# Attention: denominators of unmasked key tiles from sums made in pairs on GpSimd

## The chip, the cores and the metric

The kernel runs on one core of a Trainium2 chip. The metric is the device time of one launch in microseconds. Engines are TensorE (PE; PEld is its weight load), VectorE (DVE), ScalarE (ACT), GpSimd (POOL) and SyncE (SP), whose queue issues nearly all transfers.

## What is computed

Two blocks of a sequence model over 2 x 1024 tokens of 512 channels: a time mix, a feed-forward layer, then causal attention with 16 heads of 32 channels, then a mixture of eight experts, each followed by a layer norm. The change is in attention:

```python
scores = jnp.einsum('bhqd,bhkd->bhqk', q, k) / np.sqrt(D)
scores = jnp.where(causal, scores, -jnp.inf)
attn = jax.nn.softmax(scores, axis=-1)
out = jnp.einsum('bhqk,bhkd->bqhd', attn, v).reshape(b, t, c)
```

and, beside it, in the preparation of the experts' weights, which the reference takes as `w_gate.astype(jnp.bfloat16)` and so on.

## The kernel before

Every stage is written out by hand, one function per engine; an engine's instructions run in the order of the text, and semaphores order the engines among each other. Attention is `attend` (line 1718). It works on 8 **units**: 2 batches x 4 groups of 4 heads. The scores stand transposed: keys on partitions, queries on columns. A unit has 12 **steps** (`STEPS`, line 1725): for the first 512 queries key tiles 0 to 3 (steps 0 to 3), for the second 512 key tiles 0 to 7 (steps 4 to 11). Steps 0 to 3 and 8 to 11 meet the diagonal: they are cut to 512, 384, 256 and 128 columns and need a mask. Steps 4 to 7 are whole and unmasked.

For every step and head (`h`, four of them):

- TensorE makes scores (`scores`, line 1886, matmul L1893) into one of three banks `st`, and between them the pieces of `mx.piece` (L1286), scores of the next units whose row maxima VectorE takes (L1298, L1301).
- ScalarE takes the exponential into `pt` (`exps`, L1861), a ring of `PT` = 3 buffers of 128 x 4 x 512 floats.
- GpSimd masks the diagonal block of steps that need it (`affine_select`, L1843).
- Two steps later (`LAG` = 2) TensorE multiplies `pt` by the values into `num` and by a block of ones into `den` (`pv`, L1911); the second product sums the exponentials over the keys. A product is four matmuls of 32 rows, one per head.

At steps 3 and 11 ends a half; ScalarE copies `den` and `num` out (L1852, L1853), VectorE divides (L1937, L1940), SP stores.

Beside this the stage prepares the experts' weights for the next one (`NarrowWeights`, line 1998): 24 pieces, three per unit, each loaded as 32-bit floats (`load`, L2023), cast to bf16 by GpSimd (`narrow`, L2029) and stored (`store`, L2035). Three buffers `raw` and three `cast` go round, piece n uses buffer n % 3. SP's order in unit u (lines 1795 to 1815): the seven loads of the keys, queries and values of unit u + 2 (`mx.load`, L1256, none from unit 6 on) once the products of the unit before are done; then for each of three pieces the store of the piece of unit u - 1 and the load of that of unit u; the store of results, the rows of negated maxima for unit u + 1 (L1266), a store of results. A load waits for the cast that frees `raw`, which is one unit old; a cast waits for the load and for the store that frees `cast`. On GpSimd the three casts of a unit stand at step 4, ahead of the masks of steps 8 to 11:

```python
for s in range(NS):
    if s == TT:
        for n in range(PER_UNIT):
            narrow.narrow(pool, u * PER_UNIT + n)
    if diag(s) is None:
        continue
    pool.wait_ge(exp_done, (u * NS + s + 1) * HG)
```

Of the kernel before, what the change touches and what calls it, by code (L numbers as in the profile page):

```python
# [9 lines left out]
ALU = mybir.AluOpType  # L10
# [4 lines left out]
BF16 = mybir.dt.bfloat16  # L15
U32 = mybir.dt.uint32

P = 128
# [1699 lines left out]
def attend(nc, a, src, dst, o_out, mx, ow, result):  # L1718
# [8 lines left out]
    DIAGS = sum(j >= qc * TT for qc, j in STEPS)  # L1727
    LAST_PIECES, TURN_STEP, FRONT = 8, 9, 12
    LAG = 2
    PT = LAG + 1  # L1730
    ST = 3
    DIVIDE_CHUNKS = 4
    CHUNK = TB // DIVIDE_CHUNKS
# [3 lines left out]
    with Bench(nc, "at_") as b:  # L1737
# [13 lines left out]
        o_stored = [b.sem(f"o_stored{s}") for s in range(QC)]  # L1751
        narrow = NarrowWeights(nc, b, a)
        PER_UNIT = len(narrow.pieces) // UNITS
        out = Outcome(b, src, dst, o_out, o_stored, ow, mx, st[0], ((UNITS - 2) * NS, (UNITS - 1) * NS))
        banks = [num, mx.bank[0]], [den, mx.bank[1]], [mx.bank[2], st[0]], [st[1], st[2]]
        expert_sync, expert_gpsimd, expert_scalar, expert_tensor, expert_vector = experts(
# [68 lines left out]
        @block.gpsimd  # L1825
        def _(pool):
            pool.memset(ones[:, :], 1.0).then_inc(ones_small_set, 1)
            pool.wait_ge(ones_small_set, 1)
            mx.set_ones(pool, SLOTS - 1)
            pool.wait_ge(mx.ones_set, SLOTS)  # L1830

            for u in range(UNITS):
                for s in range(NS):
                    if s == TT:
                        for n in range(PER_UNIT):
                            narrow.narrow(pool, u * PER_UNIT + n)
                    if diag(s) is None:
                        continue
                    pool.wait_ge(exp_done, (u * NS + s + 1) * HG)
                    part = pt[:, s % PT, :, diag(s):diag(s) + P]  # L1840
                    alone(pool)

                    pool.affine_select(out=part, in_=part, compare_op=ALU.is_ge, fill=0.0, base=0,  # L1843
                                       pattern=[[0, HG], [1, P]], channel_multiplier=-1).then_inc(masked, 1)
            expert_gpsimd(pool)

        @block.scalar
        def _(act):
# [6 lines left out]
            def exps(u, s):  # L1855
                off = diag(s) or 0

                at_least(act, pv_done, u * NS + s - LAG)
                for h in range(HG):
                    act.wait_ge(scores_done, (u * NS + s) * HG + h + 1)  # L1860
                    act.activation(pt[:, s % PT, h, off:TB], st[(s * HG + h) % ST][:, off:TB], ACT.Exp,  # L1861
                                   scale=SCALE).then_inc(exp_done, 1)
# [22 lines left out]
        def _(pe):  # L1885
# [13 lines left out]
            def pv(u, s):  # L1899
                qc, kt = STEPS[s]  # L1900
                off = diag(s) or 0
                pe.wait_ge(exp_done, (u * NS + s + 1) * HG)
                if diag(s) is not None:
                    pe.wait_ge(masked, u * DIAGS + diags(s) + 1)
                if kt == 0:
                    at_least(pe, copied, (u * QC + qc) * 2)
                first, last = kt == 0, s in ENDS
                for total, lhs in ((num, None), (den, ones)):
                    for h in range(HG):
                        rows = slice(h * HD, (h + 1) * HD)  # L1910
                        mm = pe.matmul(total[rows, off:TB], vv[u % SLOTS][:, kt, rows] if lhs is None else lhs[:, :],  # L1911
                                       pt[:, s % PT, h, off:TB], start=first, stop=last, skip_group_check=True)
                mm.then_inc(pv_done, 1)

            pe.wait_ge(ones_small_set, 1)
            for g in range(UNITS * NS):
                u, s = place(g)
                if s == 0:
                    pe.wait_ge(mx.ones_set, min(u + 1, SLOTS))
                    pe.wait_ge(mx.rows_loaded, (u + 1) * 2 * DMA)  # L1920
                scores(u, s)
                if g >= LAG:
                    pv(*place(g - LAG))
                if s == TURN_STEP and u + 1 < UNITS:
                    mx.turn(pe, u + 1)
            for g in range(UNITS * NS - LAG, UNITS * NS):
# [71 lines left out]
class NarrowWeights:  # L1998
# [5 lines left out]
    def __init__(self, nc, b, a):  # L2004
# [1 line left out]
        self.gu = nc.dram_tensor("expert_gu_bf", [EXPERTS, P, 2, KT * INNER], BF16, kind="Internal").ap()  # L2006
        self.d = nc.dram_tensor("expert_d_bf", [EXPERTS, P, NM * C], BF16, kind="Internal").ap()
        self.a = a
        self.raw = [b.sb(f"raw{s}", [P, NM * C]) for s in range(self.BUFFERS)]
        self.cast = [b.sb(f"cast{s}", [P, NM * C], BF16) for s in range(self.BUFFERS)]  # L2010
        self.loaded = [b.sem(f"loaded{s}") for s in range(self.BUFFERS)]
        self.stored = [b.sem(f"stored{s}") for s in range(self.BUFFERS)]
        self.narrowed = b.sem("narrowed")
# [3 lines left out]

    def load(self, sp, n):
        e, g = self.pieces[n]
        sp.wait_ge(self.narrowed, n - self.BUFFERS + 1) if n >= self.BUFFERS else None  # L2020
        source = self.a["expert_gu"][e][:, g].rearrange("p k n -> p (k n)") if g < 2 \
            else self.a["expert_d"][e].rearrange("p m n -> p (m n)")
        sp.dma_start(self.raw[n % self.BUFFERS][:, 0:self.cols(n)], source).then_inc(self.loaded[n % self.BUFFERS], DMA)  # L2023

    def narrow(self, pool, n):
        s = n % self.BUFFERS
        pool.wait_ge(self.loaded[s], (n // self.BUFFERS + 1) * DMA)
        at_least(pool, self.stored[s], (n // self.BUFFERS) * DMA)
        pool.tensor_copy(self.cast[s][:, 0:self.cols(n)], self.raw[s][:, 0:self.cols(n)]).then_inc(self.narrowed, 1)  # L2029

    def store(self, sp, n):
# [961 lines left out]
```

## Time and profile before

| | us |
|---|---|
| median of 3 runs | 1600.88 (1598.05 to 1601.29) |
| the profiled execution | 1599.74 |
| its span, first to last instruction | 1598.0 |
| PE busy | 1489.6 (93%) |
| DVE busy | 990.5 (62%) |
| ACT busy | 613.4 (38%) |
| POOL busy | 459.8 (29%) |
| mean granted TensorE clock | 0.975 of full speed |

Attention takes the time from 939 to 1281 us of the span. All rows below are from the one profiled execution. A busy time is the union of a group's instructions. A wait in brackets is the idle time of the engine ahead of an instruction and what ended it; the share of busy time says little about who waits for whom.

### The profile page before, as it was taken

The numbers are of one execution on the slowest core, as the hardware profiler recorded it, in microseconds if no ns is written. First come the engines' busy times: TensorE is split into PE (matmuls) and PEld (weight loads), VectorE is DVE, ScalarE is ACT, GpSimd is POOL, SyncE is SP. The second block draws the span as 40 slices with busy tenths as digits, with TensorE's granted clock in tenths as the row PEclk, the third lists the DMA queues.
The fourth block names the chain that finished last, engine by engine and source line by source line (L and its number), as shares of the span: only waits on it lengthen the run. The fifth ranks groups of instructions, "written<-read, shape, count | busy, mean of one in ns | idle before, by whom it ended". The sixth has DMA issues, their size and how long they took to land. (4 is left out here: it accounts for less than half of the span.)

```text
span 1598.0 us, 22563 instructions
## 1 busy us (share of the span) xinstructions
PE 1489.6 (93%) x7696; PEld 1084.6 (68%) x7696; DVE 990.5 (62%) x1916; ACT 613.4 (38%) x1079; POOL 459.8 (29%) x385
## 2 busy tenths in 40 slices
PE   6999889999999999999998989999999898897996
PEld 4787768788888888888876764444444376674554
DVE  4977967854545554552432757777777375466664
ACT  4343444623422431341211025554555634231554
POOL 0433343302421440340432122221222224003760
PEclk9999989999999999999999989999999998998998
DMA  5111536503321430424257573666662566712336
GB/s 184 44 62 53 189 112 226 195 27 130 94 66 40 145 104 0 132 79 160 110 184 232 172 201 106 177 177 190 191 187 100 201 255 226 289 56 70 102 98 224
DMA packets 105182, 223.40 MB, mean 140 GB/s; under 512 B 9281, under 2 KB 35265, under 8 KB 104193
## 3 DMA queue, kind: packets, MB, share of 16 engines
q1 hardware_dynamic: 101344, 211.96, 40.9%
q0 software_dynamic: 3744, 10.23, 2.1%
q8 instruction: 55, 0.90, 0.2%
q14 instruction: 39, 0.31, 0.1%
HBM read 157.54 MB, written 64.36 MB: 139 GB/s over the span
## 5 line engine op out<-in xcount | busy, mean ns | idle before, releaser
L1861 ACT ACTIVATE at_pt<-at_st 128x512 f32<-128x512 f32 (+3 forms) x384 | 164.2, 497 | 140.4 <-PE at_st L1893 139.6
L898 POOL TENSOR_TENSOR ff_w_lo<-ff_raw,ff_w_hi 128x1024 fp32r<-128x1024 f32 x64 | 153.8, 2405 | 210.8 <-ACT ff_w_hi L928 210.8
L115 PE MATMUL op_bank<-ff_x_hi,ff_w_lo 128*128 128x512 f32 x512 | 200.2, 391 | 0.0
L117 PE MATMUL op_bank<-ff_x_hi,ff_w_hi 128*128 128x512 f32 x512 | 200.0, 391 | 0.0
L116 PE MATMUL op_bank<-ff_x_lo,ff_w_hi 128*128 128x512 f32 x512 | 199.9, 391 | 0.0
L1159 DVE TENSOR_TENSOR ff_h_lo<-ff_hf,ff_h_hi 128x512 f32 (+1 forms) x64 | 149.6, 2337 | 53.6 <-ACT ff_h_hi L1047 53.3
L1893 PE MATMUL at_st<-mx_qp,mx_kp 98*128 98x512 f32 (+3 forms) x288 | 104.4, 395 | 15.9 <-ACT at_pt L1861 10.6
L928 ACT ACTIVATE ff_w_hi<-ff_raw 128x1024 fp32r<-128x1024 f32 x64 | 67.8, 1061 | 118.3 <-PE op_bank L117 116.0
L115 PEld LDWEIGHTS op_bank<-ff_x_hi,ff_w_lo 128*128 128x128 f32 x512 | 96.7, 189 | 20.3
L116 PEld LDWEIGHTS op_bank<-ff_x_lo,ff_w_hi 128*128 128x128 f32 x512 | 96.7, 189 | 20.2
L117 PEld LDWEIGHTS op_bank<-ff_x_hi,ff_w_hi 128*128 128x128 f32 x512 | 96.6, 189 | 20.4
L1893 PEld LDWEIGHTS at_st<-mx_qp,mx_kp 98*128 98x128 f32 x288 | 54.8, 198 | 74.5 <-issue 34.8
L1298 DVE CUSTOM_DVE_ANT_0 mx_mx<-mx_mx,mx_mask 128x256 f32<-128x256 f32 (+3 forms) x172 | 83.0, 490 | 29.7 <-PE mx_mx L1286 28.5
L115 PE MATMUL mx_mx<-ff_down_hi,ff_h_lo 128*128 128x512 f32 x256 | 100.3, 392 | 0.0
L117 PE MATMUL mx_mx<-ff_down_hi,ff_h_hi 128*128 128x512 f32 x256 | 99.8, 390 | 0.0
L116 PE MATMUL mx_mx<-ff_down_lo,ff_h_hi 128*128 128x512 f32 x256 | 99.6, 389 | 0.0
L1151 DVE SCALAR_TENSOR_TENSOR ff_hf<-op_bank,ff_sc,ff_hf 128x512 f32<-128x512 f32 x64 | 48.0, 750 | 72.0 <-PE op_bank L117 70.5
L1843 POOL TENSOR_SCALAR_AFFINE_SELECT at_pt<-at_pt 128x512 f32<-128x512 f32 x64 | 41.3, 649 | 156.8 <-ACT at_pt L1861 156.6
L1286 PE MATMUL mx_mx<-mx_kp,mx_qp 96*128 96x512 f32 (+1 forms) x208 | 75.8, 371 | 9.9 <-DMA mx_vv<-v_tokens 4.4
L1301 DVE TENSOR_REDUCE mx_tops<-mx_mx 128x1 f32<-128x512 f32 x100 | 68.7, 687 | 24.9 <-PE mx_mx L1286 24.7
L1911 PE MATMUL at_den<-at_pt,at_ones 128*32 128x512 f32 (+3 forms) x768 | 82.9, 504 | 0.0
L1040 ACT ACTIVATE ff_hf<-op_bank,ff_sc 128x512 f32<-128x512 f32 x64 | 44.0, 688 | 82.6 <-PE op_bank L117 82.6
(450 smaller groups left out, 3352.8 us busy)
## 6 DMA issues: line engine op xcount, KB each, us to landing
ff_raw<-in_Wug SPq DMA_DIRECT2D x64, 512.0 KB, 3.6
at_raw<-in_expert_gu SPq DMA_DIRECT2D x16, 704.0 KB, 12.2
mx_qp<-q_hi SPq DMA_DIRECT2D x12, 512.0 KB, 5.6
mx_kp<-k_hi SPq DMA_DIRECT2D x12, 512.0 KB, 11.3
at_raw<-in_expert_d SPq DMA_DIRECT2D x8, 768.0 KB, 14.2
expert_gu_bf<-at_cast SPq DMA_DIRECT2D x16, 352.0 KB, 10.9
ex_e_gu<-expert_gu_bf SPq DMA_DIRECT2D x8, 704.0 KB, 8.4
tm_raw_x<-in_xT SPq DMA_DIRECT2D x4, 1024.0 KB, 6.4
```

Source lines behind the costliest of these rows:

```text
L115: pe.matmul(out, cut_l(ll), cut_r(rh), start=first, stop=False, **kw)
L116: pe.matmul(out, cut_l(lh), cut_r(rl), start=False, stop=False, **kw)
L117: return pe.matmul(out, cut_l(lh), cut_r(rh), start=False, stop=last, **kw)
L898: pool.tensor_tensor(w[j][1][:, :, :, :], raw[:, j], f32(w[j][0][:, :, :, :]), ALU.subtract)\
L928: act.activation(w[j][0][:, :, :, :], raw[:, j], ACT.Copy).then_inc(w_hi_ready, 1)
L1159: dve.tensor_tensor(h_lo[:, bass.ds(n + j, 1), :], hf[:, j:j + 1, :], f32(h_hi[:, bass.ds(n + j, 1), :]), ALU.subtract).then_inc(h_lo_read ...
L1286: pe.matmul(bank[:, 0:hi - lo], self.qp[j][0:R_MAX, h, qt * P:(qt + 1) * P], self.kp[j][0:R_MAX, h, lo:hi], start=True, stop=True).then_in ...
L1298: dve.tensor_tensor_reduce(piece, piece, self.mask[:, TB - (hi - lo):], 1.0, -3e38, ALU.add, ALU.max, out)\
L1301: dve.reduce_max(out, piece, AX.X).then_inc(self.piece_read, 1)
L1861: act.activation(pt[:, s % PT, h, off:TB], st[(s * HG + h) % ST][:, off:TB], ACT.Exp, scale=SCALE).then_inc(exp_done, 1)
L1893: pe.matmul(st[(s * HG + h) % ST][:, off:TB], kp[j][0:ROWS, h, kt * P:(kt + 1) * P], qp[j][0:ROWS, h, qc * TB + off:(qc + 1) * TB], start= ...
L1911: mm = pe.matmul(total[rows, off:TB], vv[u % SLOTS][:, kt, rows] if lhs is None else lhs[:, :], pt[:, s % PT, h, off:TB], start=first, sto ...
```

## The change

In the four unmasked steps of a unit the exponentials are no longer multiplied by ones step by step. GpSimd adds those of steps 4 and 5, and of steps 6 and 7, into one buffer `pair_sum` (128 x 4 x 512), and TensorE multiplies each sum by ones once (`total_pair`), after the products that go with step 7 and with step 10. The ring `pt` has four buffers. A mask or a new exponential may not take a buffer whose sum is still to be made: `exps` waits for `summed` from step 8 on. The second sum waits for the product of the first (`totalled`), since `pair_sum` is one buffer.

To make room, each `cast` buffer of the weights is laid over its `raw` buffer. So a load may no longer start when the cast before is done, but when the store before has landed.

```diff
--- before.py
+++ after.py
@@ -1727,7 +1727,11 @@
     DIAGS = sum(j >= qc * TT for qc, j in STEPS)
     LAST_PIECES, TURN_STEP, FRONT = 8, 9, 12
     LAG = 2
-    PT = LAG + 1
+    PT = LAG + 2
+    PAIR_STEPS = [(TT, TT + 1), (TT + 2, TT + 3)]
+    SUM_AT = {step: n for n, (_, step) in enumerate(PAIR_STEPS)}
+    TOTAL_AT = {TT + 3: 0, TT + 6: 1}
+    SUMS = len(PAIR_STEPS)
     ST = 3
     DIVIDE_CHUNKS = 4
     CHUNK = TB // DIVIDE_CHUNKS
@@ -1751,6 +1755,8 @@
         o_stored = [b.sem(f"o_stored{s}") for s in range(QC)]
         narrow = NarrowWeights(nc, b, a)
         PER_UNIT = len(narrow.pieces) // UNITS
+        pair_sum = b.sb("pair_sum", [P, HG, TB])
+        summed, totalled = b.sem("summed"), b.sem("totalled")
         out = Outcome(b, src, dst, o_out, o_stored, ow, mx, st[0], ((UNITS - 2) * NS, (UNITS - 1) * NS))
         banks = [num, mx.bank[0]], [den, mx.bank[1]], [mx.bank[2], st[0]], [st[1], st[2]]
         expert_sync, expert_gpsimd, expert_scalar, expert_tensor, expert_vector = experts(
@@ -1834,6 +1840,14 @@
                     if s == TT:
                         for n in range(PER_UNIT):
                             narrow.narrow(pool, u * PER_UNIT + n)
+                    if s in SUM_AT:
+                        n = u * SUMS + SUM_AT[s]
+                        first, second = PAIR_STEPS[SUM_AT[s]]
+                        pool.wait_ge(exp_done, (u * NS + second + 1) * HG)
+                        at_least(pool, totalled, n)
+                        pool.tensor_tensor(pair_sum[:, :, :], pt[:, first % PT, :, :], pt[:, second % PT, :, :], ALU.add)\
+                            .then_inc(summed, 1)
+                        pool.wait_ge(summed, n + 1)
                     if diag(s) is None:
                         continue
                     pool.wait_ge(exp_done, (u * NS + s + 1) * HG)
@@ -1855,7 +1869,9 @@
             def exps(u, s):
                 off = diag(s) or 0
 
-                at_least(act, pv_done, u * NS + s - LAG)
+                at_least(act, pv_done, u * NS + s - PT + 1)
+                if s >= 2 * TT:
+                    act.wait_ge(summed, u * SUMS + (s - 2 * TT) // 2 + 1)
                 for h in range(HG):
                     act.wait_ge(scores_done, (u * NS + s) * HG + h + 1)
                     act.activation(pt[:, s % PT, h, off:TB], st[(s * HG + h) % ST][:, off:TB], ACT.Exp,
@@ -1906,11 +1922,20 @@
                     at_least(pe, copied, (u * QC + qc) * 2)
                 first, last = kt == 0, s in ENDS
                 for total, lhs in ((num, None), (den, ones)):
+                    if lhs is not None and TT <= s < 2 * TT:
+                        continue
                     for h in range(HG):
                         rows = slice(h * HD, (h + 1) * HD)
                         mm = pe.matmul(total[rows, off:TB], vv[u % SLOTS][:, kt, rows] if lhs is None else lhs[:, :],
                                        pt[:, s % PT, h, off:TB], start=first, stop=last, skip_group_check=True)
                 mm.then_inc(pv_done, 1)
+
+            def total_pair(u, n):
+
+                pe.wait_ge(summed, u * SUMS + n + 1)
+                for h in range(HG):
+                    mm = pe.matmul(den[h * HD:(h + 1) * HD, :], ones[:, :], pair_sum[:, h, :], start=n == 0, stop=False, skip_group_check=True)
+                mm.then_inc(totalled, 1)
 
             pe.wait_ge(ones_small_set, 1)
             for g in range(UNITS * NS):
@@ -1921,6 +1946,8 @@
                 scores(u, s)
                 if g >= LAG:
                     pv(*place(g - LAG))
+                if s in TOTAL_AT:
+                    total_pair(u, TOTAL_AT[s])
                 if s == TURN_STEP and u + 1 < UNITS:
                     mx.turn(pe, u + 1)
             for g in range(UNITS * NS - LAG, UNITS * NS):
@@ -2006,8 +2033,12 @@
         self.gu = nc.dram_tensor("expert_gu_bf", [EXPERTS, P, 2, KT * INNER], BF16, kind="Internal").ap()
         self.d = nc.dram_tensor("expert_d_bf", [EXPERTS, P, NM * C], BF16, kind="Internal").ap()
         self.a = a
-        self.raw = [b.sb(f"raw{s}", [P, NM * C]) for s in range(self.BUFFERS)]
-        self.cast = [b.sb(f"cast{s}", [P, NM * C], BF16) for s in range(self.BUFFERS)]
+        homes = []
+        self.raw = []
+        for s in range(self.BUFFERS):
+            homes.append(b.next_at())
+            self.raw.append(b.sb(f"raw{s}", [P, NM * C]))
+        self.cast = [b.overlay(f"cast{s}", [P, NM * C], homes[s], BF16) for s in range(self.BUFFERS)]
         self.loaded = [b.sem(f"loaded{s}") for s in range(self.BUFFERS)]
         self.stored = [b.sem(f"stored{s}") for s in range(self.BUFFERS)]
         self.narrowed = b.sem("narrowed")
@@ -2017,7 +2048,7 @@
 
     def load(self, sp, n):
         e, g = self.pieces[n]
-        sp.wait_ge(self.narrowed, n - self.BUFFERS + 1) if n >= self.BUFFERS else None
+        at_least(sp, self.stored[n % self.BUFFERS], n // self.BUFFERS * DMA)
         source = self.a["expert_gu"][e][:, g].rearrange("p k n -> p (k n)") if g < 2 \
             else self.a["expert_d"][e].rearrange("p m n -> p (m n)")
         sp.dma_start(self.raw[n % self.BUFFERS][:, 0:self.cols(n)], source).then_inc(self.loaded[n % self.BUFFERS], DMA)
@@ -2025,7 +2056,6 @@
     def narrow(self, pool, n):
         s = n % self.BUFFERS
         pool.wait_ge(self.loaded[s], (n // self.BUFFERS + 1) * DMA)
-        at_least(pool, self.stored[s], (n // self.BUFFERS) * DMA)
         pool.tensor_copy(self.cast[s][:, 0:self.cols(n)], self.raw[s][:, 0:self.cols(n)]).then_inc(self.narrowed, 1)
 
     def store(self, sp, n):
```

GpSimd's order in the first unit, from the memset of the constant rows of `kp` to the masks of the second half. The names are the tiles of attention (`at_`); of before:

```order
L1843 AFFINE_SELECT at_pt<-at_pt 128x4x128 x4
L2029 CAST at_cast<-at_raw 128x1408 x2
L2029 CAST at_cast<-at_raw 128x1536
L1843 AFFINE_SELECT at_pt<-at_pt 128x4x128 x8
L2029 CAST at_cast<-at_raw 128x1408 x2
```

and of the change:

```order
L1857 AFFINE_SELECT at_pt<-at_pt 128x4x128 x4
L2059 CAST at_cast_7012<-at_raw 128x1408
L2059 CAST at_cast_7013<-at_raw 128x1408
L2059 CAST at_cast_7014<-at_raw 128x1536
L1848 TENSOR_TENSOR at_pair_sum<-at_pt 128x2048 x2
L1857 AFFINE_SELECT at_pt<-at_pt 128x4x128 x8
```

Both sums stand behind the three casts and ahead of the mask of step 8.

TensorE from the last scores of step 8 to the first piece behind the turned maxima in step 10 (`at_st` are scores, `mx_mx` and `at_mx` pieces); of before:

```order
L1911 MATMUL at_num<-at_pt,mx_vv 32x512 x4
L1911 MATMUL at_den<-at_pt,at_ones 32x512 x4
L1893 MATMUL at_st<-mx_qp,mx_kp 128x384 x4
L1911 MATMUL at_num<-at_pt,mx_vv 32x512 x4
L1911 MATMUL at_den<-at_pt,at_ones 32x512 x4
L1311 MATMUL mx_mx<-mx_ident,mx_tops 32x128
```

and of the change, the end of step 7 and then the same place:

```order
L1929 MATMUL at_num<-at_pt,mx_vv 32x512 x4
L1937 MATMUL at_den<-at_pair_sum,at_ones 32x512 x4
L1909 MATMUL at_st<-mx_qp,mx_kp 128x512
...
L1909 MATMUL at_st<-mx_qp,mx_kp 128x384 x4
L1929 MATMUL at_num<-at_pt,mx_vv 32x512 x4
L1311 MATMUL mx_mx<-mx_ident,mx_tops 32x128
```

The products with ones behind steps 4 to 7 are gone, and the product over the first sum stands between steps 7 and 8.

## Rows read from the trace of the kernel before

**Rows 1.** the page, part 2: busy tenths of TensorE in 40 equal slices.

```profile
PE   6999889999999999999998989999999898897996
```

**Rows 2.** who waited for whom, 939 to 1281 us: us, times, longest us.

```profile
PE at_st L1893 <- ACT at_pt L1861: 12.5, 31, 2.7
PE at_st L1893 <- POOL at_ones L1827: 5.0, 1, 5.0
...
ACT at_pt L1861 <- PE at_st L1893: 139.6, 101, 4.5
```

**Rows 3.** timeline of SP, units 2, 3 and 7: start, us, issue.

```profile
1035.27 0.33 SPq L1256 DMA_DIRECT2D mx_qp<-q_hi  x1
...
1038.98 6.26 SPq L2035 DMA_DIRECT2D expert_gu_bf<-at_cast  x1
...
1047.51 0.43 SPq L2023 DMA_DIRECT2D at_raw<-in_expert_d  x1
...
1077.59 0.32 SPq L1256 DMA_DIRECT2D at_qp<-q_hi  x1
...
1238.65 0.50 SPq L2035 DMA_DIRECT2D expert_gu_bf<-at_cast  x1
```

**Rows 4.** timeline of TensorE, units 0, 2 and 7.

```profile
970.12 0.50 PE L1893 MATMUL at_st<-mx_qp,mx_kp 98*128 98x512 f32 x1
...
1051.02 1.04 PE L1911 MATMUL at_den<-at_pt,at_ones 128*32 128x512 f32 x8
1051.99 0.50 PE L1893 MATMUL at_st<-at_qp,at_kp 98*128 98x512 f32 x1
...
1055.67 0.50 PE L1893 MATMUL at_st<-at_qp,at_kp 98*128 98x512 f32 x1
...
1066.05 1.06 PE L1911 MATMUL at_num<-at_pt,at_vv 128*32 128x512 f32 x8
...
1267.46 0.73 PE L1893 MATMUL at_st<-mx_qp,mx_kp 98*128 98x512 f32 x2
```

**Rows 5.** timeline of GpSimd, units 0, 2 and 6: last column the wait before.

```profile
968.43 1.47 POOL L2029 CAST at_cast<-at_raw 128x1536 bf16<-128x1536 f32 x1 [0.48 <-DMA at_raw<-in_expert_d]
...
1057.61 1.36 POOL L2029 CAST at_cast<-at_raw 128x1408 bf16<-128x1408 f32 x1 [16.36 <-DMA at_raw<-in_expert_gu]
...
1062.97 1.47 POOL L2029 CAST at_cast<-at_raw 128x1536 bf16<-128x1536 f32 x1 [1.39 <-DMA at_raw<-in_expert_d]
1064.39 1.22 POOL L1843 TENSOR_SCALAR_AFFINE_SELECT at_pt<-at_pt 128x512 f32<-128x512 f32 x2
...
1212.14 4.07 POOL L2029 CAST at_cast<-at_raw 128x1408 bf16<-128x1408 f32 x3
```

**Rows 6.** groups by form of GpSimd, whole span: busy us, mean ns.

```profile
L898 POOL TENSOR_TENSOR ff_w_lo<-ff_raw,ff_w_hi 128x1024 fp32r<-128x1024 f32 x64 | 153.8, 2405 | 210.8 <-ACT ff_w_hi L928 210.8
...
L352 POOL TENSOR_TENSOR tm_rw<-tm_num,tm_rec 128x512 f32<-128x512 f32 x16 | 28.7, 1796 | 79.9 <-DVE tm_rec L585 79.9
...
L2297 POOL TENSOR_TENSOR ex_sd_lo<-ex_raw_d,ex_sd_hi 128x1536 fp32r<-128x1536 f32 x1 | 3.5, 3479 | 0.0
```

**Rows 7.** DMA issues of 1038.9 to 1040 us: KB, us to landing.

```profile
expert_gu_bf<-at_cast SPq DMA_DIRECT2D x1, 352.0 KB, 16.9
```

**Rows 8.** DMA issues of unit 6 from 1197.7, then of unit 7 from 1238.6.

```profile
at_raw<-in_expert_gu SPq DMA_DIRECT2D x1, 704.0 KB, 5.1
expert_gu_bf<-at_cast SPq DMA_DIRECT2D x1, 352.0 KB, 2.9
...
expert_gu_bf<-at_cast SPq DMA_DIRECT2D x1, 352.0 KB, 9.4
```

**Rows 9.** the page, part 6: DMA issues.

```profile
ff_raw<-in_Wug SPq DMA_DIRECT2D x64, 512.0 KB, 3.6
```

**Rows 10.** busy time in two stretches: PE, PEld, DVE, ACT, POOL, PEclk, DMA.

```profile
938.00:951.00 13.00, 12.70 (x44) 8.55 (x44) 8.46 (x28) 6.98 (x13) 5.55 (x5) 0.50 0.90 216
1108.00:1113.00 5.00, 4.98 (x24) 1.75 (x23) 3.49 (x10) 0.88 (x3) 0.63 (x1) 0.66 0.15 56
```

## The prediction

> **What bounds the kernel now.** I first read the page's slices [rows 1]: TensorE is busy in eight tenths or more of every slice but the first and two of the last four, also in attention (939 to 1281 us, slices 24 to 33 of 40). TensorE bounds that stage, as far as it has operands. The lists of waits there [rows 2] say that its longest is for the exponentials, 12.5 us in 31 waits; GpSimd is waited for once, 5.0 us at the stage's start. ScalarE waits 139.6 us for scores, in its group of exponentials, and for nothing else of weight. Then I read one unit in time, unit 2 (of 0 to 7), and count from T0, the issue of its first load of keys and queries, 1035.27 [rows 3]; the next unit's is 1077.59, so a unit takes 42.3 us.
>
> In the TensorE timeline [rows 4] a group of products with ones over 512 columns (one matmul per head, four; the row counts eight) starts at 1051.02, and the scores behind it at 1051.99: 0.97 us a group. Scores of step 8 start at 1055.67, T0+20.4. In the GpSimd timeline [rows 5] the three casts of a unit, which stand ahead of all it does from step 4 on, do not follow the mask of step 3. The first starts at 1057.61 after 16.36 us of waiting for its weight piece, and the third ends at 1064.44, T0+29.2. Only then come the masks of steps 8 and 9, which TensorE needs at 1066.05 [rows 4]. So GpSimd is idle a long time and yet **late**, because DMA is late. Nothing waits for it today, by 1.6 us.
>
> **The products.** Per unit four groups with ones go (4 x 0.97 = 3.9 us) and two over the sums come (1.9): 1.9 us saved, 15.5 us in eight units. This is all that can be gained; the fourth buffer for exponentials gives nothing, since ScalarE waits for scores and not for a buffer [rows 2].
>
> **The sums on GpSimd.** No row has an add of 128 x 2048. The nearest: 128x1536 in 3479 ns and 128x1024 in 2405 [rows 6]. The slope between them, 2.10 ns a column, gives 3479 + 512 x 2.10 = 4.55 us; 2.35 ns a column gives 4.8. I take 4.7. The upper end is the two-operand multiply, 1796 ns for 512 columns [rows 6], 7.2 us for 2048. The first sum comes behind the three casts, and TensorE's product over it stands between step 7 and step 8, so step 8 begins no earlier than casts + 4.7 + 1.0. Even with today's casts this would be T0+34.9 in place of T0+20.4.
>
> **The loads.** Each cast is now laid over its raw piece, so a load waits until the store out of the same buffer has landed, and that store was issued just before it. On SP's queue store 0, wait, load 0, store 1, wait, load 1, store 2, wait, load 2 follow each other; today all six are issued by T0+12.7 (1047.51 and its 0.43, [rows 3]) and queue together. What stands behind them on SP (the rows of negated maxima, the stores of results) is needed only later in the unit. Store 0 is issued at 1038.98 behind seven loads of 512 KB and lands 16.9 us later [rows 7], T0+20.6; worked out alike the five units 1 to 5 give 19.2 to 20.6, mean 20.0. From there the queue is empty. In unit 6, where no loads of keys stand ahead, a store landed after 2.9 us, and the load issued 0.48 us behind it after 5.1 [rows 8], the pair 5.6 us from first issue. A round (load k with store k+1 behind it) I therefore take at 5.6, and the last load alone at 5.1: 5.6 + 5.6 + 5.1 = 16.3, so the last piece is there at T0+36.3 instead of T0+27.7 (1062.97, [rows 5]). Lower end: 512 KB in 3.6 us [rows 9] and 0.7 more for 704 KB (at 2.7 us per 704 KB), 4.3 a round with the store hidden in it, 13.1 in all, T0+33.1. Upper end: 7.4 a round, T0+42.
>
> As to the page's rule: the Trainium skill ("DMA: Bandwidth & Descriptors", section on the anatomy of one DMA) puts a transfer at about 2.0 us fixed plus bytes over 436 GB/s. By that estimate a round is 4.5 us and the chain 12.9; the pair in rows 8 took 5.6, so the rows speak for the longer one.
>
> **The sum for a unit.** Last piece T0+36.3, cast 1.5, sum 4.7 with 0.1 for the hand-overs, product 1.0: step 8 begins at T0+43.6, 23.2 us late. Behind it two groups with ones fewer and one over the second sum, 1.0 less: **+22.2**. The second sum starts after the first product and ends 4.9 us into step 8; the exponentials of step 10 come about 7.7 after step 8's start and its masked product 10.4 after [rows 4], so it is hidden, its mask too. If the second sum took 7.2 it would only just be.
>
> TensorE then stands idle for some 25 us in each of these units (from T0+18.5; the products saved before that are lost in the wait). Before the attention stage it stood idle 5.0 us [rows 2], and the granted clock was 0.50 in the 13 us behind it [rows 10], that is 1.2 GHz instead of 2.4, with TensorE busy 12.7 of 13 us. Elsewhere (1108 to 1113, [rows 10]) the clock was 0.66 over 5 us with hardly a pause, a loss of 2. Half of 5 to 13 us is 2.4 to 6.4 us lost per unit; I take 4. Per unit **+26.2, in five units +131**.
>
> Unit 0 has no stores ahead of its loads. The third cast starts at 968.43 [rows 5], ends at 969.9; 4.7, 0.1 and 1.0 bring step 8 to 975.7 instead of 970.12 [rows 4]: +5.6 - 1.0 = 4.6, with 2.4 for the clock +7. Unit 6 has an empty queue: casts begin at 1212.14 without a wait [rows 5], its chain ends some 16 us after 1200.7, and the sum is there before step 8: -2. Unit 7: store issued 1238.65 [rows 3], lands 9.4 later [rows 8], plus 16.3 + 1.5 + 4.8 + 1.0 is 1271.6 against step 8 at 1267.46 [rows 4]: +4 - 1 = +3.
>
> 131 + 7 - 2 + 3 = **+139**. The profiled execution took 1599.74 us (span 1598.0); the sum gives 1739. The median of the runs, 1600.88, is 1.1 above that execution, less than I can resolve.
>
> **Rivals.**
> *Short rounds* (chance 0.11): DMA rounds at the 4.3 us bound. Same mechanism, 3.2 us less in five units: 1723. Rows 9 speak for it, rows 8 against. It is also where the skill's rule above would lead.
> *The loads are not held* (0.06): the store has landed whenever SP comes to the load, casts end at T0+29.2 as now. Step 8 is 14.5 late, less 1.0, plus 4 for the clock: 17.5 x 5 + 8 = +95, 1695. Against it: the store of rows 7 lands at 1055.88, when even the last of today's loads has long been issued (1047.51, [rows 3]), and the load must now come behind it.
> *Heavier* (0.09): the sum at 7.2, rounds near 7, the clock low for 13 us each time: up to 37 a unit, 1760 to 1790.
> *Faster* (0.03): both sums are done when TensorE comes to them, and only the saving stays: 1600 - 15.5 = 1584. This is one condition in one place, that the first sum starts by T0+13, 4.8 and a margin ahead of TensorE's arrival at T0+18.5; it needs the last weight piece some 15 us sooner than it lands today in five of eight units. GpSimd is idle enough for it (16.36 us before the first cast, [rows 5]), but that idle time is a wait at the head of its queue. Only unit 6, whose pieces need no wait, comes near the condition.
> That the change doesn't do what it says is excluded by the order of instructions shown above: the groups with ones are gone and the sums are there. I give 0.01 to no change.
>
> **The numbers.** The forecast, 1739, has 0.70. The range for 8 in 10 holds it with its bounds (clock 2.4 to 6.4 a unit, rounds from 4.3) and the rivals of the same mechanism, and leaves out the unheld loads, the faster case and the far end of the heavier: 1700 to 1780. A difference of 0.2% (3 us) is about what a measurement of this kernel tells from none. Faster 0.03, same 0.01, slower 0.96.
>
> **What would show it.** In the changed profile: SP's issues of weight loads 5 to 6 us apart, not 1; the third cast at about T0+36 in units 1 to 5; the adds at 4.6 to 4.8 us; a TensorE wait of some 25 us in each of them, ended by the add on GpSimd, at the product over the sum; PEclk at 0.5 behind it; units of 65 to 69 us instead of 42.3; the stages before and behind attention unchanged. It is wrong if the third cast stays at T0+27.7 (the loads are not held), if the add takes 7 us, or if the clock stays at 1.00 after the wait. If GpSimd's wait before its casts has shrunk, the cover that I deny is there.

## The result and the profile after

The changed kernel takes 1745.66 us (median of 4 runs, 1735.65 to 1748.47), the kernel before beside it 1601.09: ratio 1.089, 95% interval 1.084 to 1.094. The forecast was 1739. The profiled execution has a span of 1746.7 us and a mean clock of 0.926.

The page after, the rows that answer to [rows 1], and the group of the new products:

```profile
PE   6999889999999999999988848549458888987997
...
PEclk9999999999999999999998968779677889998999
...
L1937 PE MATMUL at_den<-at_pair_sum,at_ones 128*32 128x512 f32 x128 | 23.5, 818 | 127.7 <-POOL at_pair_sum L1848 127.7
```

TensorE's busy digits now fall to 4 and 5 where they were 9, and the granted clock falls with them. The last column of the group is most of the story in one number: TensorE idles 127.7 us ahead of the products over sums, of the 148.7 us by which the span grew. The mean of one matmul, 818 ns, lies above the 592 ns that it takes where the clock is full.

Who waited for whom in attention, 939 to 1428 us, TensorE (answers to [rows 2]):

```profile
PE at_den L1937 <- POOL at_pair_sum L1848: 127.7, 7, 23.9
PE at_st L1909 <- ACT at_pt L1877: 11.3, 26, 2.7
PE mx_mx L1286 <- DVE mx_tops L1298: 5.0, 10, 3.3
```

The timeline of SP in unit 2 and the first issue of unit 3 (start, us; answers to [rows 3]):

```profile
1068.19 0.33 SPq L1256 DMA_DIRECT2D mx_qp<-q_hi  x1
...
1072.54 6.20 SPq L2065 DMA_DIRECT2D expert_gu_bf<-at_cast  x1
1087.89 0.34 SPq L2054 DMA_DIRECT2D at_raw<-in_expert_gu  x1
1088.28 0.43 SPq L2065 DMA_DIRECT2D expert_gu_bf<-at_cast  x1
1093.48 0.33 SPq L2054 DMA_DIRECT2D at_raw<-in_expert_gu  x1
1093.86 0.43 SPq L2065 DMA_DIRECT2D expert_d_bf<-at_cast  x1
1099.01 0.33 SPq L2054 DMA_DIRECT2D at_raw<-in_expert_d  x1
...
1135.52 0.33 SPq L1256 DMA_DIRECT2D at_qp<-q_hi  x1
```

GpSimd in the same unit (answers to [rows 5]):

```profile
1092.65 1.36 POOL L2059 CAST at_cast<-at_raw 128x1408 bf16<-128x1408 f32 x1 [18.47 <-DMA at_raw<-in_expert_gu]
1098.06 1.36 POOL L2059 CAST at_cast<-at_raw 128x1408 bf16<-128x1408 f32 x1 [4.05 <-DMA at_raw<-in_expert_gu]
1103.96 1.47 POOL L2059 CAST at_cast<-at_raw 128x1536 bf16<-128x1536 f32 x1 [4.54 <-DMA at_raw<-in_expert_d]
1105.39 4.50 POOL L1848 TENSOR_TENSOR at_pair_sum<-at_pt 128x2048 f32<-128x2048 f32 x1
1112.08 4.55 POOL L1848 TENSOR_TENSOR at_pair_sum<-at_pt 128x2048 f32<-128x2048 f32 x1 [2.19 <-PE at_den L1937]
```

TensorE (answers to [rows 4]), the product over the first sum and the scores of step 8 behind it:

```profile
1109.94 1.94 PE L1937 MATMUL at_den<-at_pair_sum,at_ones 128*32 128x512 f32 x8 [22.99 <-POOL at_pair_sum L1848]
1111.81 0.79 PE L1909 MATMUL at_st<-at_qp,at_kp 98*128 98x512 f32 x1
```

Read the three together from T0 = 1068.19: the first load is let go at T0+19.7, the next two 5.6 and 5.5 us later; the third cast starts at T0+35.8; the sum follows at once, and TensorE, idle since T0+18.8, goes on at T0+41.8. GpSimd's wait for the first piece did not shrink (18.47 us, before 16.36 [rows 5]): the cover that the forecast denied isn't there.

Busy time in stretches of that unit (PE, PEld, DVE, ACT, POOL, PEclk, DMA share, GB/s):

```profile
1087.00:1110.00 23.00, 0.06 (x4) 0.06 (x8) 0.54 (x1) 0.00 (x0) 8.65 (x4) 0.58 0.48 142
1110.00:1117.00 7.00, 7.00 (x24) 2.81 (x24) 3.46 (x8) 2.39 (x4) 4.76 (x2) 0.50 0.00 0
1117.00:1126.00 9.00, 7.92 (x52) 3.37 (x48) 5.76 (x16) 3.38 (x9) 1.70 (x3) 0.95 0.02 5
```

The clock is at 1.2 GHz (0.50) when TensorE comes back, and is given again only some 7 us into the work.

A unit's length, from its first mask on GpSimd to the next unit's (unit 7: to the end of the last exponential):

| unit | before | after | difference | predicted |
|---|---|---|---|---|
| 0 | 48.3 | 54.3 | +6.0 | +7 |
| 1 to 5 | 213.3 | 343.3 | +130.0 | +131 |
| 6 | 38.6 | 43.8 | +5.2 | -2 |
| 7 | 36.6 | 44.8 | +8.2 | +3 |

The sum, 149.4, is the difference of the two spans (1746.7 and 1598.0, 148.7): outside attention nothing moved. Unit 6 is the surprise. There the first sum runs on GpSimd from 1353.35 to 1357.88, beside this work of VectorE, and TensorE waits for the maxima (`mx_tops`) that stand behind it in VectorE's order:

```profile
1353.35 4.53 POOL L1848 TENSOR_TENSOR at_pair_sum<-at_pt 128x2048 f32<-128x2048 f32 x1 [2.05 <-ACT at_pt L1877]
...
1353.67 0.95 DVE L1964 RECIPROCAL at_den_sb<-at_den_sb 128x128 f32<-128x128 f32 x1
1354.66 3.78 DVE L1967 TENSOR_TENSOR at_num_sb<-at_num_sb,at_den_sb 128x512 f32<-128x512 f32 x1
...
1358.76 0.80 PE L1286 MATMUL mx_mx<-mx_kp,mx_qp 96*128 96x512 f32 x1 [3.29 <-DVE mx_tops L1298]
```

The division of the unit before (a multiply by the reciprocals, 128 x 512) took 3.78 us. In the kernel before, VectorE's division and its maximum that joins the halves of the maxima take:

```profile
1048.69 0.69 DVE L1940 TENSOR_TENSOR at_num_sb<-at_num_sb,at_den_sb 128x512 f32<-128x512 f32 x1
...
1058.90 0.18 DVE L1306 TENSOR_TENSOR mx_tops<-mx_tops 128x16 f32<-128x16 f32 x1
```

So the division took 3.1 us longer than before the change, and the 3.3 us wait of TensorE for `mx_tops` comes from it.

### The profile page after: what moved, and what is told of

It reads as the page before. It is cut to its first block and busy times, and to the rows that moved or that the text cites. A ratio compares the mean times of both kernels' runs of the same rounds, so it can differ in the third digit from the quotient of the medians.

```text
span 1746.7 us, 22316 instructions
## 1 busy us (share of the span) xinstructions
PE 1509.2 (86%) x7568; PEld 1091.8 (63%) x7568; DVE 1007.3 (58%) x1916; ACT 616.2 (35%) x1079; POOL 537.2 (31%) x401
## 5 line engine op out<-in xcount | busy, mean ns | idle before, releaser
L1937 PE MATMUL at_den<-at_pair_sum,at_ones 128*32 128x512 f32 x128 | 23.5, 818 | 127.7 <-POOL at_pair_sum L1848 127.7
L1909 PE MATMUL at_st<-mx_qp,mx_kp 98*128 98x512 f32 (+3 forms) x288 | 113.1, 426 | 15.1 <-ACT at_pt L1877 9.7
L1909 PEld LDWEIGHTS at_st<-mx_qp,mx_kp 98*128 98x128 f32 x288 | 59.5, 215 | 83.1 <-issue 39.2
L1298 DVE CUSTOM_DVE_ANT_0 mx_mx<-mx_mx,mx_mask 128x256 f32<-128x256 f32 (+3 forms) x172 | 83.1, 489 | 29.1 <-PE mx_mx L1286 27.7
L1301 DVE TENSOR_REDUCE mx_tops<-at_mx 128x1 f32<-128x512 f32 x28 | 19.3, 690 | 136.2 <-PE at_mx L1286 135.4
L1937 PEld LDWEIGHTS at_den<-at_pair_sum,at_ones 128*32 128x32 f32 x128 | 4.0, 132 | 140.9 <-POOL at_pair_sum L1848 134.1
L1286 PE MATMUL mx_mx<-mx_kp,mx_qp 96*128 96x512 f32 (+1 forms) x208 | 79.5, 389 | 12.1 <-DMA mx_vv<-v_tokens 4.4
```

The lines of the kernel that those rows point to most:

```text
L1286: pe.matmul(bank[:, 0:hi - lo], self.qp[j][0:R_MAX, h, qt * P:(qt + 1) * P], self.kp[j][0:R_MAX, h, lo:hi], start=True, stop=True).then_in ...
L1298: dve.tensor_tensor_reduce(piece, piece, self.mask[:, TB - (hi - lo):], 1.0, -3e38, ALU.add, ALU.max, out)\
L1909: pe.matmul(st[(s * HG + h) % ST][:, off:TB], kp[j][0:ROWS, h, kt * P:(kt + 1) * P], qp[j][0:ROWS, h, qc * TB + off:(qc + 1) * TB], start= ...
```

## The experiments

Two theories. **A, the loads**: the time is the chain store, load, cast, sum, product, as forecast. **B, the sum itself**: GpSimd's sum holds up VectorE while it runs, so that it would cost time even if the chain were short. The first four kernels ran where the kernel before took 1626 us, the next four where it took 1624, the last three where it took 1600. So ratios are compared, and the length of attention from the first exponential's start to the last one's end: 339.4 us before, 488.7 after. That length comes from one profiled execution of each kernel. A second execution of the changed kernel (further down) has 479.7, so it is good to some 9 us where the waits are long; 140 us more than before, in that execution, is what the ratio says too (0.089 x 1600 = 142).

### Both parts of the change apart

The kernel before with the casts laid over their raw buffers, and no sums (the edit shortened; a filler of the freed size keeps all later buffers in their places):

```diff
-            self.raw.append(b.sb(f"raw{s}", [P, NM * C]))
-        self.cast = [b.sb(f"cast{s}", ...) ...]
+        self.cast = [b.overlay(f"cast{s}", [P, NM * C], homes[s], BF16) ...]
-        sp.wait_ge(self.narrowed, ...)
+        at_least(sp, self.stored[n % self.BUFFERS], n // self.BUFFERS * DMA)
```

> The kernel before, with the casts laid over their raw pieces and the loads waiting for the stores, and nothing of the sums. Theory (the held loads and the sums each cost, one behind the other): the third cast ends at about T0+37.7 in units 1 to 5, as in the changed kernel, so the mask of step 8 comes at T0+38.4 and TensorE, which wants it at T0+30.8, waits 7 to 8 us in each of the five units, and loses some 3 more to the lower clock: 1600 + 5 x 8 to 11 = 1640 to 1655. Rival 1 (all of the loss is of the sums): 1601. Rival 2 (all of it is of the held loads): about 1740.

Measured: 1673.32 us, ratio 1.029 (1.025 to 1.033), attention 386.1 us, +47. The units 1 to 5 take 52.3 us on the mean. TensorE's waits:

```profile
PE at_num L1911 <- POOL at_pt L1843: 37.9, 5, 8.4
```

The waits are now for the masks behind the late casts, as expected: the held loads alone cost a third of the loss.

The other part: the changed kernel with casts of their own and the old wait for the loads. The room for the sum is lent from the output weights' places, which are free until unit 7; in unit 7 the sum takes another place there, with one wait more on GpSimd and one on ScalarE. The edit, shortened:

```diff
+        self.cast = [b.sb(f"cast{s}", [P, NM * C], BF16) for s in range(self.BUFFERS)]
-        pair_sum = b.sb("pair_sum", [P, HG, TB])
+        sums = [b.overlay("pair_sum_w", [P, HG, TB], ow.weights_at), ...]
```

> The changed kernel with three cast buffers of their own and the old waits; the sum buffer is lent from the output weights' places. Theory: casts end at T0+29.2 as before the change, the first sum at T0+33.8 instead of T0+42.2, and the 8.4 us are gained whole in five units, since the sum is what TensorE waits for either way: 1746 - 42 = 1704. Rival 1 (held loads are all of it): 1585 to 1600. Rival 2 (held loads don't matter): 1746.

Measured: 1709.81, ratio 1.053 (1.048 to 1.058), attention +86. Units of 57.7 us. GpSimd in the unit whose T0 is 1057.11:

```profile
1084.78 1.47 POOL L2060 CAST at_cast<-at_raw 128x1536 bf16<-128x1536 f32 x1 [1.40 <-DMA at_raw<-in_expert_d]
1086.21 4.49 POOL L1851 TENSOR_TENSOR at_pair_sum_w<-at_pt 128x2048 f32<-128x2048 f32 x1
```

The third cast is at T0+27.7, where it is in the kernel before, and TensorE still waits (79.7 us in 6 times). So the loads' hold is not needed for a loss: the sum behind casts that come as early as before costs 15 us a unit (57.7 against 42.7 before), the hold alone 10 us (52.3), together 25 of the 26 seen (68.7). The gain against the changed kernel, 54 to 63 us in attention and 57 by the ratios, is larger than the 42 expected: the third cast starts 8.7 us earlier in a unit on the mean, near the 8.4 worked out, and the units are shorter by 10 to 11.

### The sum taken off the casts

The changed kernel, loads held as in it, but the casts behind the mask of step 11, so that no sum waits for them:

```diff
-                    if s == TT:
+                    if u == UNITS - 1 and s == 2 * TT:
                         for n in range(PER_UNIT):
                             narrow.narrow(pool, u * PER_UNIT + n)
...
+                    if u < UNITS - 1 and s == NS - 1:
+                        for n in range(PER_UNIT):
+                            narrow.narrow(pool, u * PER_UNIT + n)
```

> The changed kernel with one edit in GpSimd's order: the three casts of a unit stand behind the mask of step 11 (in the last unit ahead of the mask of step 8). The sums are then made in time, at T0+12 to 16.6 and T0+19.4 to 24. Theory A (the casts ahead of the sums are the whole loss): the unit takes 1.9 us less than before the change, 1585 to 1590. Theory B (an add on GpSimd also holds up VectorE instructions that read two operands from SBUF, as the changed kernel's unit 6 shows, 3.78 us for 0.69, with TensorE waiting 3.3 us for VectorE and then at the lower clock): 5 to 6 us more in each unit, 1630 to 1650.

Measured: 1660.71, ratio 1.023 (1.019 to 1.027), attention +37, units of 47.9 us. The waits for sums are gone, but theory A's saving does not come. TensorE's longest wait, and VectorE's groups in attention (busy, mean ns):

```profile
PE mx_mx L1286 <- DVE mx_tops L1298: 20.9, 12, 3.3
```

```profile
L1970 DVE TENSOR_TENSOR at_num_sb<-at_num_sb,at_den_sb 128x512 f32<-128x512 f32 x15 | 28.9, 1929 | 0.5
...
L1306 DVE TENSOR_TENSOR mx_tops<-mx_tops 128x16 f32<-128x16 f32 x7 | 10.7, 1525 | 0.2
```

The sum in one unit, and the division that starts 1.29 us into it:

```profile
1051.04 4.54 POOL L1848 TENSOR_TENSOR at_pair_sum<-at_pt 128x2048 f32<-128x2048 f32 x1 [6.16 <-ACT at_pt L1880]
```

```profile
1052.33 3.79 DVE L1970 TENSOR_TENSOR at_num_sb<-at_num_sb,at_den_sb 128x512 f32<-128x512 f32 x1
```

1052.33 + 3.79 = 1056.12, and the sum ends at 1055.58: the multiply of 0.69 us doesn't finish until the sum is over. Theory B has a place: the maxima of the next unit queue behind that instruction, and TensorE queues behind them. Next, the same with the division of a unit's second half moved to step 9 of the next unit, beside no sum:

```diff
-                if chunk == DIVIDE_CHUNKS - 1:
+                if chunk == DIVIDE_CHUNKS - 1 and (qc == 0 or u == UNITS - 1):
...
                 if s == TURN_STEP:
+                    if u:
+                        divide(u - 1, 1)
```

> late_casts with one more edit, on VectorE: the product of numerator and inverted denominator of a unit's second half stands at step 9 of the next unit instead of step 5, away from the first sum. Theory B: the first sum meets no instruction with two SBUF operands, the second one only the small join of the maxima (under 2 us, not waited for): 1585 to 1600. If other VectorE instructions are held up as well, or the loss is elsewhere: as late_casts. Theory A: equal to late_casts at 1585 to 1590.

Measured: 1638.27, ratio 1.009 (1.006 to 1.012), attention +13. The division is back at 683 ns and TensorE no longer waits for the maxima, yet the expectation of a kernel faster than before failed. A wait stands in the place of the one removed:

```profile
PE at_st L1912 <- issue: 12.8, 4, 4.2
```

Another, of 5.0 us, is there in both of these runs: in unit 7 their casts stand ahead of the mask of step 8 (its product at 1286.78 waits for that mask).

Scores of step 0 need the rows of negated maxima. SP issues them behind the held loads:

```profile
1026.69 0.33 SPq L2063 DMA_DIRECT2D at_raw<-in_expert_d  x1
1027.07 0.43 SPq L1797 DMA_DIRECT2D attended<-at_num_sb  x1
1027.54 0.51 SPq L1266 DMA_DIRECT2D at_qp<-mx_neg_hi  x1
1028.10 0.60 SPq L1266 DMA_DIRECT2D at_qp<-mx_neg_lo  x1
```

The last of these rows lands 4.9 us after its issue at 1028.10, and TensorE starts at 1033.06 after 4.23 us. The store of results between them and the loads didn't hold them up: its division had ended at 1019.34. With units this short the hold reaches a step that it could not reach before.

### All three moved, and the control

Casts with places of their own, behind step 11's mask in units 0 to 5 (in units 6 and 7 at step 4 as before), and the division at step 9.

> The sums with both costs taken away: the casts have places of their own (their loads wait for no store), they run behind the mask of step 11 in units 0 to 5, and VectorE divides the second half of a unit at step 9 of the next one. Nothing of the computation changes. My theory (held loads, plus VectorE's two-operand instruction held while a sum runs, are the whole cost; the product over ones saves 1.9 us a unit): no wait of TensorE for the first sum above 1 us, the division at 0.7 us, no rows of maxima late at step 0 (they were 4.2 us late where the loads were held too), and most of 15.5 us saved: ratio to the kernel before 0.990 to 0.998. Rival, the rows of maxima are late for another reason than the held loads, or the sums hold up TensorE anyway: 1.006 or more, as with the late casts and the moved division.

> Control for the run with everything moved: the kernel before with the same two moves (casts behind the mask of step 11 in units 0 to 5, division of the second half at step 9 of the next unit), no sums. Both moves are of work that is off the critical path in the kernel before, so the ratio is 0.998 to 1.002. If it is below that, a gain of the run with everything moved is not the sums'; if above, the moves cost something by themselves.

Measured: with the sums 1611.94 against 1624.22, ratio **0.9926** (0.990 to 0.995), attention 328.8 us, 10.6 less than before; the control, the same moves without sums, 1624.29, ratio 0.9998 (0.9985 to 1.0011). Units 1 to 5 take 204.3 us with the sums, 213.3 before and 214.1 in the control: 1.8 to 2.0 saved a unit, the 1.9 of the products. The control's attention, on the slower chip, takes 338.3 us against 339.4: the 24 us between those chips lie outside attention. TensorE's waits in attention are the small ones of before:

```profile
PE at_st L1916 <- ACT at_pt L1883: 13.7, 32, 2.7
PE mx_mx L1286 <- ACT mx_neg_hi L1316: 4.1, 6, 0.7
```

So once nothing waits for the sums a unit from 1 to 6 gains what its products save, no part of the loss is left, and the moves by themselves neither cost nor gain. Units 0 and 7 gain nothing (48.4 against 48.3 us, 36.9 against 36.6, and 35.3 in the control's unit 7), which is why it is 12 us and not 15.5; their reason was not looked for. The 128 x 16 maximum that joins the halves (L1306) is still held up, 1515 ns a time.

### The sizes: clock, rounds, sum, unit 6

TensorE kept at work during its wait:

```diff
+                if n == 0 and 1 <= u <= 5:
+                    pe.wait_ge(exp_done, (u * NS + 2 * TT) * HG)
+                    for _ in range(95):
+                        pe.matmul(st[0][:, :], kp[...], qp[...], start=True, stop=True)
```

> The changed kernel; in units 1 to 5 TensorE runs 95 further matmuls of 512 columns (some 21 us) into a score buffer that is free, in front of the wait for the first sum. What they write is overwritten unread. My theory: the 4.5 us by which a unit's end is longer than at full clock are the clock of 0.5 after TensorE has been idle for some 23 us, so the clock stays near 1.0 behind the sum and five units are 4.5 us shorter: 22 us less, ratio to the kernel before about 1.075 where the changed kernel has 1.089. Rival, the end of the unit is set by ScalarE or VectorE and the clock is beside the point: 1.089 as without the matmuls.

Measured: 1756.42 beside 1624.22, ratio 1.084 (1.080 to 1.088); units 1 to 5 take 322.5 us. Stretches of unit 2, the matmuls and behind them:

```profile
1082.00:1104.00 22.00, 21.28 (x94) 17.27 (x92) 0.11 (x1) 0.00 (x0) 6.58 (x4) 1.00 0.50 148
1104.00:1112.00 8.00, 5.52 (x32) 2.55 (x36) 4.03 (x8) 3.34 (x8) 6.68 (x2) 1.00 0.00 0
1112.00:1120.00 8.00, 6.95 (x50) 3.08 (x42) 6.96 (x19) 2.91 (x9) 1.89 (x4) 1.00 0.11 37
```

The clock stays at 1.00. From the start of the first sum to the next T0 each of units 1 to 4 takes 26.6 us; in the changed kernel it takes 30.1 in three of them and 32.2 in one, in its second execution 28.0 to 33.8. The clock costs 3.5 to 5.6 us a unit in the one and 1.4 to 7.2 in the other, on the mean 4.0 and 3.4. By the ratios alone this isn't settled (1.084 and 1.0885 have intervals that overlap, and the expected 1.075 was not reached); that a unit's end is shorter at full clock is read from the traces.

The stores issued first, then the loads:

```diff
                 for n in range(PER_UNIT):
                     if u:
                         narrow.store(sp, (u - 1) * PER_UNIT + n)
+                for n in range(PER_UNIT):
                     narrow.load(sp, u * PER_UNIT + n)
```

> The changed kernel; SyncE issues the three stores of the narrow weights one after the other and then the three loads, instead of store, load, store, load, store, load. My theory: the rounds are long because each store has to end before the next load is let go, and each round pays both latencies; with the stores overlapped the third piece arrives about 3.5 us earlier (at 32.7 us of the unit instead of 36.2), and every unit from 1 to 5 is 3.5 us shorter: 17 us less, ratio about 1.078. Rival, the three rounds are set by bytes, so that the order of issue does not matter: 1.089, with the third cast still 36 us into the unit.

Measured: ratio 1.062 (1.059 to 1.064), attention 436.8 us: 52 less than the changed kernel in its first execution and 43 in its second. By the ratios it is 0.0268 x 1600 = 43, two and a half times what was expected. The unit with T0 = 1058.74:

```profile
1077.99 1.23 SPq L2055 DMA_DIRECT2D at_raw<-in_expert_gu  x2
1079.82 0.49 SPq L2055 DMA_DIRECT2D at_raw<-in_expert_d  x1
```

```profile
1082.95 1.36 POOL L2060 CAST at_cast<-at_raw 128x1408 bf16<-128x1408 f32 x1 [18.23 <-DMA at_raw<-in_expert_gu]
1085.63 1.36 POOL L2060 CAST at_cast<-at_raw 128x1408 bf16<-128x1408 f32 x1 [1.32 <-DMA at_raw<-in_expert_gu]
1087.50 1.47 POOL L2060 CAST at_cast<-at_raw 128x1536 bf16<-128x1536 f32 x1 [0.51 <-DMA at_raw<-in_expert_d]
```

All three loads are let go within 1.8 us and the pieces come 2.7 and 1.9 us apart; one after the other they came 5.4 and 5.9 apart. The third cast is at T0+28.8, not 32.7. So each piece but the first comes 2.7 to 4.0 us sooner behind the one before it than in a round. The stores, which ran beside the loads in the rounds and now go ahead of them, are part of that difference; what they and what the waiting for one another contribute was not separated.

The first sum made twice:

```diff
+                        if SUM_AT[s] == 0:
+                            pool.tensor_tensor(pair_sum[:, :, :], ..., ALU.add).then_inc(again, 1)
+                            pool.wait_ge(again, u + 1)
```

and the changed kernel beside it, and the changed kernel with the division moved (the edit shown above):

> The changed kernel itself beside the other runs on this chip, for the comparison with the run with further matmuls (1.084) and with the stores issued first (1.062). If those two gained 20 us and 52 us in the attention stage, as their traces say against the trace of the changed kernel, this comes out at 1.089 to 1.096; if it is 1.085 or less, the further matmuls gained nothing.

> The changed kernel with GpSimd making the first sum of each unit twice in succession, the second time with the same inputs into the same place (nothing of the output changes). My theory: the sum stands at the end of the chain store, load, cast, sum, product in units 0 to 5 and 7, so each of these seven units takes a further 4.5 us: 32 us more than the changed kernel, and some more where TensorE's clock falls for longer: ratio to the kernel before 1.109 to 1.115. Rival, GpSimd has room for the sums and only the loads set the time: 1.089 to 1.095, as the changed kernel.

> The changed kernel with one thing moved: VectorE divides the second half of a unit at step 9 of the next unit, as in the earlier run with that move. In units 1 to 5 the first sum comes so late that the division was never beside it (0.69 us each), so nothing changes there. In unit 6 no store holds the loads, the sum began while VectorE was about to divide, and the division took 3.78 us. My theory: unit 6 is 4 to 7 us shorter (44 us in the changed kernel), and all else stays: ratio 0.002 to 0.004 below the changed kernel's. Rival, what is late in unit 6 is something else: its length and the ratio stay.

| kernel | ratio (95%) | units 1 to 5, us | unit 6, us |
|---|---|---|---|
| changed, again | 1.0885 (1.0855 to 1.0915) | 337.1 | 44.4 |
| first sum twice | 1.109 (1.106 to 1.112) | 360.3 | 44.5 |
| division moved | 1.083 (1.080 to 1.086) | 333.7 | 36.6 |

The second making of the sum costs 0.0204 x 1600 = 33 us, as expected, at the lower end of the ratio; in unit 6, whose first sum isn't at the end of the chain, it costs nothing. With the division moved unit 6 goes from 44.4 to 36.6 us, more than the 4 to 7 expected, and 2.0 under the 38.6 of before. Two executions of the changed kernel differ by 6 us in units 1 to 5, so no more than unit 6 is read from the ratio 1.083, which fell by more than the 0.002 to 0.004 expected.

## Why the prediction was right, and where it was not

- **The products**, 1.9 us a unit: right. With every wait gone 1.8 remained; a group over a sum takes 1.04 us at full clock.
- **The sum on GpSimd**, 4.7 taken from the slope or the rate of two forms: 4.49 to 4.58, but for 4.93 once. The slope's 4.55 was the better reading; the multiply's 7.2 was no near row.
- **The loads**: right in mechanism and place. The first load goes at T0+19.7 to 20.7 (20.0 forecast), rounds of 5.6 and 5.5 (5.6 forecast), third cast in units 1 to 5 at T0+35.8 to 36.7 (36.3). The pair of load and store in rows 8 gave the round; the estimate of 4.5 us from the Trainium skill ("DMA: Bandwidth & Descriptors", section "Anatomy of one DMA — SWDGE (gpsimd) path") was 1.1 short. That section gives its fit for transfers issued from GpSimd, and these were issued from SyncE.
- **The margin today**: "Nothing waits for it today, by 1.6 us" was read from the end of the casts. The mask of step 8 stands between (half of the 1.22 us of two masks in rows 5), so it is 1.0. The sum doesn't use it.
- **Step 8** at T0+43.6: measured 1111.81 - 1068.19 = 43.6. The wait of some 25 us is 23.
- **The clock**, 4 us a unit from 2.4 to 6.4: 4.0 and 3.4 on the mean of the two executions, by the run with matmuls in the wait; single units lie between 1.4 and 7.2. The 0.66 over 5 us that stood for the other end is a loss of 1.7, not 2.
- **Unit 0**, +7: +6.0. **Units 1 to 5**, +131: +130.0, and +123.8 in the second execution. That the first is 1 us off is luck: two executions differ by six times as much.
- **Unit 6**, -2: +5.2. Here the step failed: "its chain ends some 16 us after 1200.7, and the sum is there before step 8: -2." The sum is there in time. The term put at nothing is what the sum costs while it runs: the forecast names no engine that it could hold up. It holds up VectorE: the division is held for 3.1 us, TensorE waits 3.3 for the maxima queued behind it, and works at half clock after that:

```profile
1353.00:1360.00 7.00, 3.31 (x24) 1.58 (x16) 6.96 (x12) 3.31 (x7) 4.53 (x1) 0.77 0.10 37
1360.00:1366.00 6.00, 6.00 (x24) 2.78 (x20) 3.20 (x9) 2.31 (x4) 0.00 (x0) 0.50 0.01 2
1410.00:1428.00 18.00, 17.63 (x80) 5.77 (x76) 9.44 (x11) 8.12 (x20) 7.36 (x6) 0.58 0.04 16
```

With the division elsewhere the -2 is there (36.6 against 38.6).
- **Unit 7**, +3: +8.2 in one execution and, with 39.8 us, +3.2 in the other. The last stretch above is unit 7's: 0.58 over 18 us, a loss which the forecast did not reckon there. In the other execution the clock is 0.91 over the same part (1402 to 1420 us). Its spread between executions is as large as the miss.
- **The total**, +139: 148.7 in the first execution, and 140.3 of attention in the second. The second fits so well because two misses cancel there, units 1 to 5 (7 under the forecast) and unit 6 (8 over).
- The rival *the loads are not held* (1695) gave T0+29.2 for the casts' end and 17.5 us a unit. Measured without the hold: 15 a unit, ratio 1.053, which is 1685 us.
- The rival *faster* (1584) asked that the first sum start by T0+13. It named the casts as the only obstacle. Two more stood behind them: VectorE held up, and the rows of maxima. With all three gone it is 0.9926, or 1588 us on 1600.

VectorE's hold, which the forecast did not see, costs 7 to 8 us here (unit 6), because in the other units the sums come too late to meet the division; where the casts are out of the way it costs 24 (attention 376.0 and 352.3 us).

## What to carry to other kernels

Ask of every instruction put on an idle engine what stands ahead of it in that engine's queue, and when the data of that one arrives: GpSimd was 29% busy, and yet its first cast stood waiting for a piece for some 16 us in each of units 1 to 5. When a buffer is laid over another to make room, the wait that it brings moves to the queue that loads it, and reaches all that stands behind; issue all that frees before all that waits. Removing the longest wait shows the next one, so price a chain of fixes only as a whole: here the first fix took 104 to 113 us off the attention stage and the second 24, and only the third, with 23.5, brought a gain over the kernel before.

## What the runs showed of the hardware

A VectorE instruction that reads two operands from SBUF doesn't finish while GpSimd adds two operands from SBUF: 3.78 and 3.79 us for 0.69 (128 x 512), ending 0.56 and 0.54 us after the sum, and 1.65 for 0.18 (128 x 16), ending 0.03 us after it. The last is from the run with only the division moved, in unit 6:

```profile
1350.98 4.58 POOL L1848 TENSOR_TENSOR at_pair_sum<-at_pt 128x2048 f32<-128x2048 f32 x1 [2.87 <-PE at_den L1937]
...
1353.94 1.65 DVE L1306 TENSOR_TENSOR mx_tops<-mx_tops 128x16 f32<-128x16 f32 x1
```

A reciprocal with one SBUF operand, started inside the same sum as the 3.78, took its 0.95 us. The Trainium skill, "SBUF — State Buffer", section "Who interferes with whom", says that a VectorE instruction with two SBUF inputs contends with a GpSimd instruction that reads SBUF, that what they share is an exclusive lock, and that the order of issue decides who blocks. These rows agree; the page could have given the term for unit 6.

TensorE idle for 23 us comes back at the lower of its two clock levels, 1.2 GHz, and stays there for some 7 us of dense work; with 95 matmuls of 512 columns in the wait it stays at 2.4 GHz throughout. After the 3.3 us wait in unit 6 the clock was at the lower level too, 0.50 over the 6 us from 1360 to 1366.
